# Preparing the walk over groups of 256 edges: one table of triples and 7 gathers for three tables and 21, links turned on TensorE, stores by single transfers

## The reference, cut to what matters

```python
edge_index = jnp.stack([src, dst])          # 200000 edges, dst sorted
alpha = leaky_relu(a_s[src] + a_d[dst], 0.2)
amax = segment_max(alpha, dst)              # softmax over the edges of one dst
e = exp(alpha - amax[dst]); z = segment_sum(e, dst)
out = segment_sum(xh[src] * (e / (z[dst] + 1e-16)), dst) + bias
```

## Time and profile before

| | |
|---|---|
| median of 3 runs | 7640.53 us |
| lowest and highest of them | 7630.43 and 7646.57 us |
| profiled execution, its own time | 7630.02 us |
| its span, first to last instruction | 7628.1 us |
| POOL, DVE, PE busy | 68%, 66%, 72% |

### The profile page before, as it was taken

How to read it: one execution, slowest core, us unless ns; L and a number is a source line. 1 busy time by engine, 2 the same in 40 slices (tenths; PEclk the granted TensorE clock), 3 DMA queues, 4 the chain that set the end, 5 groups by cost and what they waited for, 6 DMA issues and landing times. The chain is left out here.

```text
span 7628.1 us, 113689 instructions
## 1 busy us (share of the span) xinstructions
PE 5472.0 (72%) x23859; PEld 3659.4 (48%) x23860; DVE 5062.0 (66%) x13667; ACT 2560.3 (34%) x7905; POOL 5154.9 (68%) x5441
## 2 busy tenths in 40 slices
PE   3577777777666577777777776578888877774399
PEld 1254544544444355555544444355555544443398
DVE  4466666666667577777766667567777776668643
ACT  1322222222222333334332222344444432222466
POOL 1577777777774677777777773677777777772444
PEclk6777777777778777777777677677778777776599
DMA  4555555545453444444444444444444444444444
GB/s 117 160 145 141 145 144 142 145 136 140 139 139 101 121 120 121 123 123 122 123 116 112 112 111 117 125 124 126 129 127 128 129 120 112 112 111 128 150 70 64
DMA packets 547396, 947.74 MB, mean 124 GB/s; under 512 B 127840, under 2 KB 380808, under 8 KB 546759
## 3 DMA queue, kind: packets, MB, share of 16 engines
q0 software_dynamic: 260256, 691.84, 34.5%
q1 hardware_dynamic: 283255, 247.26, 10.9%
q10 hardware_dynamic: 3296, 2.36, 0.1%
HBM read 794.88 MB, written 149.50 MB: 124 GB/s over the span
## 5 line engine op out<-in xcount | busy, mean ns | idle before, releaser
L1213 POOL DMA_INDIRECT edges_G<-rows,edges_index x4980 | 4720.9, 948 | 1660.0 <-issue 1485.0
L1425 PE MATMUL edges_ps_o<-edges_G,edges_OH 128*128 128x264 f32 x9960 | 3542.1, 505 | 1233.2 <-DVE acc L1684 1230.3
L1425 PEld LDWEIGHTS edges_ps_o<-edges_G,edges_OH 128*128 128x128 f32 x9960 | 2300.0, 248 | 2009.3 <-DVE acc L1684 1394.9
L1263 ACT ACTIVATE edges_OHT<-edges_ps_far 128x512 bf16<-128x512 f32 x1245 | 741.0, 595 | 2305.0 <-PE edges_ps_far L1385 2304.9
L1666 DVE TENSOR_TENSOR edges_G<-edges_G,edges_ps_c 128x1024 f32<-128x1024 f32 x1245 | 1503.0, 1207 | 0.0
L1684 DVE TENSOR_TENSOR acc<-acc,edges_ps_o 128x264 f32 x2490 | 1059.8, 426 | 296.7 <-DVE acc L1684 161.6
L1565 DVE TENSOR_TENSOR edges_tu<-edges_ad,edges_G 128x80 f32<-128x80 f32 x249 | 75.0, 301 | 1252.5 <-DMA edges_G<-rows,edges_index 1252.5
L1658 DVE TENSOR_TENSOR edges_OH<-edges_ps_c,relT 128x512 f32<-128x512 f32 x1245 | 845.3, 679 | 0.6 <-ACT edges_ps_c L1240 0.5
L1385 PE MATMUL edges_ps_far<-edges_rels,pole_rows 5*128 5x512 bf16 x1245 | 608.4, 489 | 328.0 <-ACT edges_OHT L1263 285.3
L1385 PEld LDWEIGHTS edges_ps_far<-edges_rels,pole_rows 5*128 5x128 bf16 x1245 | 117.3, 94 | 959.4 <-issue 497.7
L1232 ACT ACTIVATE edges_node<-terms 128x12 bf16 x2490 | 476.2, 209 | 142.5 <-issue 88.4
(11 more groups left out here) (360 smaller groups left out, 6073.1 us busy)
## 6 DMA issues: line engine op xcount, KB each, us to landing
edges_G<-rows,edges_index POOLq DMA_INDIRECT x4980
xslot<-edges_blank SPq DMA_DIRECT2D x80, 650.0 KB
edges_masks<-lanes SPq DMA_DIRECT2D x249, 96.0 KB
rows<-node_ext SPq DMA_DIRECT2D x147, 130.0 KB, 2.3
experts_X<-xslot SPq DMA_DIRECT2D x105, 130.0 KB, 2.1
node_rows<-rows SPq DMA_DIRECT2D x98, 130.0 KB, 2.3
h<-node_Hn SPq DMA_DIRECT2D x98, 128.0 KB, 1.7
W<-in_L_ffn_W SPq DMA_DIRECT2D x16, 512.0 KB
```

The lines of the kernel that those rows point to most:

```text
L1213: g.indirect_dma_start(G[n][:, s, 0:RW], None, dr["rows"], bass.IndirectOffsetOnAxis(index[n][:, s:s + 1], 0)).then_inc(gathered[n], 16)
L1263: a.activation(OHT[:, 4 * k:4 * k + 4, :].rearrange("p s e -> p (s e)"), ps_far[:, :], ACT.Relu, bias=1.0, scale=-1.0).then_inc(oht_ready, 1)
L1425: mm = pe.matmul(ps_o[BANK_OF[g]][:, 0:GW], OH[:, 2 * g + j, :], G[n][:, 2 * g + j, :], start=(j == 0), stop=(j == 1))
```

## The change

The walk is rewritten in these points.

- `dstI` is loaded straight from the input `dst`, in three transfers, with no wait for a padded table.
- ACT's queue, which had nothing to do in this phase, builds one table `triples` of 783 rows, each 256 `dst`, 256 `dst` shifted by one and 256 `src` (3 KB a row), by ten transfers. POOL waits for them as well before it gathers, and issues 7 gathers of 3 KB a row into `Tg`.
- `ps_col` is no longer summed: DVE copies row 0 of `ps_row` out, and PE turns it by 7 matmuls of one column.
- DVE reads the gathered integers without the casts of both `dst` parts. The lanes' last flags (`edge_ends`) are turned on PE (4 transposes), so that `links` lies on 7 partitions with 256 numbers in a row.
- `cont`, `links`, `lanes` and `powers` are stored by one or two transfers each, `lanes` and `powers` on ACT's queue. `powers` lies in DRAM by group now, so that each edge window's `rels` load reads 30 pieces of 512 bytes in place of 3 of 5 KB.

```diff
+            sp.dma_start(dstI[:, 0:TC - 1, :], dst[0:full * GE].rearrange("(c p e) -> p c e", p=P, e=GE)).then_inc(dst_in, 16)
...
+            sp.dma_start(dr["cont"][1:1 + GC * GE].rearrange("(c p) -> c p", p=GE), links[:, 0, 1, :]).then_inc(cont_out, 16)
+            sp.wait_ge(cont_out, 32)
+            sp.dma_start(links[:, 1, 1, :], dr["cont"][0:GC * GE].rearrange("(c p) -> c p", p=GE)).then_inc(cont_in, 16)
             sp.wait_ge(links_ready, 2)
             for k in range(2):
-                for m in range(2):
-                    for c, n in chunks():
-                        sp.dma_start(by_lane(dr["links"][k, m, :], c, n), links[0:n, k, m, c, :]).then_inc(walk_out, 16)
+                sp.dma_start(dr["links"][k].rearrange("m (c p) -> c m p", p=GE), links[:, k, :, :]).then_inc(walk_out, 16)
...
+        @block.scalar
+        def _(a):
+            for m, (of, o) in enumerate(sources):
+                a.dma_start(triples[0:whole, m, :], of[o:o + whole * GE].rearrange("(t e) -> t e", e=GE)).then_inc(edges_in, 16)
...
+            a.wait_ge(lanes_ready, 3)
+            a.dma_start(dr["lanes"].rearrange("(c p j) x -> p c (j x)", p=P, j=2), lanes[:, :, :, :, :].rearrange("p c j m e -> p c (j m e)")
+                        ).then_inc(walk_out, 16)
...
+            g.wait_ge(edges_in, 16 * 10)
             g.wait_ge(index_ready, 1)
             for c in range(GC):
...
+                g.indirect_dma_start(Tg[:, c, :, :].rearrange("p a b -> p (a b)"), None, triples.rearrange("t a b -> t (a b)"),
+                                     bass.IndirectOffsetOnAxis(grpI[:, c:c + 1], 0)).then_inc(rows_in, 16)
...
+            for r in range(HALVES):
+                v.tensor_copy(row_grp[:, r * rowT:(r + 1) * rowT], ps_row[0:1, r, 0:rowT]).then_inc(row_ready, 1)
...
-            for m in range(GC):
-                for c in range(TC):
-                    mm = pe.matmul(ps_col[:, m:m + 1], passed[:, c, m * P:(m + 1) * P], ones[:, 0:1],
-                                   start=(c == 0), stop=(c == TC - 1))
             mm.then_inc(walked, 1)
+            pe.wait_ge(row_ready, 1 + HALVES)
+            for m in range(GC):
+                mm = pe.matmul(ps_col[:, m:m + 1], row_grp[:, m * P:(m + 1) * P], st["ident"][0:1, 0:1], start=True, stop=True)
+            mm.then_inc(row_turned, 1)
...
-                sp.dma_start(rels[r:r + 3, :], dr["powers"][:, bass.ds(w * WS * P, WS * P)]).then_inc(rels_in[w % 2], 16)
+                sp.dma_start(rels[r:r + 3, :].rearrange("k (v e) -> k v e", e=GE), dr["powers"][bass.ds(w * WG, WG), :, :].rearrange("v k e -> k v e")).then_inc(rels_in[w % 2], 16)
```

More of the change, by code:

```diff
@@ L127, in prepare_walk @@
     pad_rows = TG + 1
+    whole = E // GE
+    rest = E - whole * GE
+    assert 1 < rest < GE and whole + 1 == TG
     with Phase(nc, "walk") as ph:
-        pads = pad_rows * GE - E
-        cut = (E - 1) // 16 * 16
-        pad = ph.sb("pad", [1, 3, pads + 1], I32)
+        pad = ph.sb("pad", [1, 3, GE], I32)
         dstI = ph.sb("dstI", [P, TC, GE], I32)
@@ L195, in prepare_walk @@
         block = ph.block()
[L196 to L210, removed]
+        HALVES = 2
+        rowT = NG // HALVES
@@ L212, in _ @@
+        assert NG % HALVES == 0 and rowT <= 512
+        triples = dr["triples"]
+        sources = ((dst, 0), (dst, 1), (src, 0))
         @block.sync
         def _(sp):
[L214 to L224, removed]
@@ L234, in _ @@
+            sp.dma_start(dstI[whole - full:whole - full + 1, TC - 1, 0:rest], dst[whole * GE:E].rearrange("(a e) -> a e", a=1)
+                         ).then_inc(dst_in, 16)
             sp.wait_ge(pole_ready, 3)
@@ L248, in _ @@
[L248 to L255, removed]
@@ new lines, in _ @@
+            lane = lanes[:, :, :, :, :]
+            by_lane = nodes.rearrange("p c (j e) -> p c j e", j=2)
+            v.tensor_scalar(lane[:, :, :, 0, :], last[:, :, :].rearrange("p c (j e) -> p c j e", j=2), -BIG, None, ALU.mult
+                            ).then_inc(lanes_ready, 1)
+            for j in range(2):
+                for m, edge in ((1, 0), (2, P - 1)):
+                    v.tensor_tensor(lane[:, :, j, m, :], by_lane[:, :, j, :], by_lane[:, :, j, edge:edge + 1].broadcast_to([P, GC, P]),
+                                    ALU.is_equal).then_inc(same, 1)
@@ new lines, in _ @@
+            v.wait_ge(same, 4)
+            for m in (1, 2):
+                v.tensor_scalar(lane[:, :, :, m, :], lane[:, :, :, m, :], 1.0, BIG, ALU.subtract, ALU.mult).then_inc(lanes_ready, 1)
+            v.memset(before[:, :], -BIG).then_inc(cont_ready, 1)
+            v.wait_ge(lanes_ready, 3)
+            for m in range(2):
+                v.tensor_copy(edge_ends[:, m, :, :].rearrange("p j c -> p c j"), lane[:, :, :, m, P - 1]).then_inc(ends_ready, 1)
+            v.wait_ge(rows_ready, 3)
```

167 lines of the change are left out of this document (74 added, 93 removed).

## The result

| | before | after |
|---|---|---|
| median, lowest, highest of 6 runs | 7640.85, 7630.43, 7646.57 us | 7579.46, 7571.98, 7584.42 us |
| profiled execution: own time, span | 7630.02, 7628.1 us | 7579.77, 7578.0 us |
| next phase begins at | 125.45 us | 67.58 us |

The change takes 0.992 of the time before, 95% interval [0.991, 0.9929]. The forecast was 7579, the range 7565 to 7600.

The account below looks back on a forecast made before the run. POOL's gathers pace the edge phases, untouched by the change; the walk's 125 us, one chain, are all there is to win. Terms sum to -57.7 us, put on the mean 7636.9: 7579, range 7565 to 7600.

Parts of the forecast that it names:

- the load of `dstI`: Start of the walk: issued first, sharing engines evenly with the table copies, DVE begins at 9.3 for 16.08; -6.8 us.
- to the first gather: From DVE's first cast to POOL's first gather: pole rows moved, 49 column matmuls gone, copies and 7 matmuls added; -0.1 us.
- the table: ACT's copies of the triples land at 13 to 16 us, before gathers at 22.4; cost 0. Rival, late table: 7586, chance 0.08.
- the gathers: Walk, 7 gathers for 21 at POOL's 1.25 us each: 11.5 us for 28.8, -17.3. Rival, by bytes: 7596, chance 0.08.
- DVE on the rows: DVE's work after the gathers: two casts of 1.0 us go, small operations of 1.4 us come; net -0.6 us.
- the shifted links: DVE's idle wait for `cont` stored and loaded back: the lag of 4-byte pieces and the idle time go; -8.2 us.
- the end: From DVE's last copy to the next phase: stores land before DVE ends, 1.9 us remain of 26.6; -24.7 us.
- The upper bound: Load of `dstI`: DVE begins at 16.08, as now, if the load has to let all the table copies go first.
- 0.2 for two more hand-overs: Part of the stretch to the first gather: 0.2 us added for two more hand-overs.
- small stores stay slow: Rival: any small store to DRAM keeps the 9.4 us lag, DVE idles 4.4 us for the links; 7585, chance 0.22.
- 830 pieces against 8: Argument against slow small stores: `cont` went out in 830 4-byte pieces, now 7 rows of 512 bytes and one number.
- Later: Edge phases: `rels` loads of 30 pieces for 3 in each of 249 windows are hidden by a whole window; cost nothing.

Follow-up runs that it names:

- the later session: The change once more, unedited, beside the kernel before on the same chip: 7587.37 us, 0.9928 of 7643.65.
- 768 rows: The change with each large copy of the table cut into one of 768 rows and one of 13: 8951.07 us in one run, beside 9015.13 before.
- the kernel of 21 gathers: The change with three tables of 1 KB rows for one of triples, so 21 gathers: 7596.11 us, 0.9955 of 7630.11.
- 1792 pieces of 512 bytes: The change with ACT's shares, turns moved up, ACT doing all 42 copies, `powers` stored in three parts, a memset after POOL's table wait: 8949.19 us, 0.9928 of 9015.13.
- the old layout: The change with `powers` stored as before by three transfers, and three `rels` pieces a window: 7587.46 us, 0.9924.

## Why the prediction was right, step by step

The profiled executions of before and after, each stretch by its two ends:

| step | forecast | measured |
|---|---|---|
| the load of `dstI` (16.08 to 6.77) | -6.8 | -9.3 |
| to the first gather (13.22 to 14.19) | -0.1 | +1.0 |
| the table | 0 | 0 |
| the gathers (28.78 to 12.76) | -17.3 | -16.0 |
| DVE on the rows (23.35 to 23.39) | -0.6 | 0.0 |
| the shifted links (8.23 of idle time) | -8.2 | -8.2 |
| the 42 copies (9.19 to 9.37, with the last add) | 0 | +0.2 |
| the end (26.6 to 1.10) | -24.7 | -25.5 |
| sum | -57.7 | -57.9 |

The total is right to 0.2 us in the walk, and each of the large terms comes from the mechanism that was forecast, but the total flatters the sum: three terms were off by 1 to 2.5 us, and cancel. That the median is met to 0.5 us is luck. The medians lie 61.4 us apart, the profiled spans 50.1 and the two medians of the later session 56.3, and the change's own runs spread over 12 and 22 us.

**The load of `dstI`.** Taken in the middle of its bounds, by an even split with the copies, at 9.3; it was 6.77, near the lower bound of 6.3. "If the engines split their time evenly" did not hold, since the copies kept to 11 of the 16 engines (by their 0.69 of the rate of 768 rows). With 768 rows the cast came at 8.20, so up to 1.4 of the 2.5 us are that. The other 1.1 were there with 16 engines too, and what they come from isn't shown. The upper bound was a real one: with long packets in the copies it was 12.69.

**To the first gather.** The seven turns were priced at 1.33 from the upper row and took 1.72. "0.2 for two more hand-overs" was the step that failed: POOL's first gather now waits for the table and the index both, and that alone cost 0.6.

**The table.** It had landed by 16.07, the upper edge of the 13 to 16, 4.9 us before it was needed. The windows show copies that keep to 0.69 of what they reach with 768 rows (265 and 386 GB/s). The rule of the Trainium skill that the prediction weighed, 11 engines for 781 rows, is borne out by that, and the table came a microsecond ahead of the estimate by it. That it still landed near the sum's own 13 to 16 is two errors that cancel: 11 engines carried the copies where 16 were counted, and a piece took some 46 ns of an engine where 57 were (an estimate from the windows: 265 GB/s at a share of 0.75, and 386 at 1.09, give the same). As the prediction says, it left the sum alone; that it would help the load was not seen.

**The gathers.** POOL's pace was right (1.25 from the third gather on, 24.18 to 29.21), and so was the remark that the bytes lie close. They lay closer to binding than the 11.5 us had it. The windows of the changed kernel late in the gathers:

```profile
26.00:28.00 2.00, 0.00 (x0) 0.00 (x0) 0.00 (x0) 0.00 (x0) 1.39 (x3) 0.50 0.81 261
...
30.00:32.00 2.00, 0.00 (x0) 0.00 (x0) 0.00 (x0) 0.00 (x0) 0.16 (x1) 0.50 0.91 320
```

The share climbs to 0.91 and stays there when POOL has issued its last (29.21 and 0.95), and with rows of 1 KB (the kernel of 21 gathers) the tail is 3.1 us: the 1.1 us by which it grew (4.5 for 3.42) are bytes. The first two gathers, 3.2 us from the first's start to the third's for 2.5, give the rest.

**DVE on the rows.** The new cast of `Sf` reads every third run of `Tg` and takes 2.01 us, where the cast of a whole tile takes 1.09. The prediction counted casts by number, not by the form of their source. That is 0.9 us; the operations that were added took some 1.0 us and not 1.4, which gives part of it back.

**The shifted links and the end.** Both lags went, as the landing of 512-byte rows took 1.3 us, and the rival "small stores stay slow" was wrong: its 2-byte store did not lag. But the argument against it, the count ("830 pieces against 8"), is only half of the reason. The lag does not shrink from 3320 pieces to 830, and 1792 pieces of 512 bytes did not have it, so the count alone does not explain it. The end took 1.1 and not 1.9 us: `powers` and `links` had landed, and the earlier trace rows was read at too late a row. The first instruction of the phase that begins there is not DVE's at 252.85 but this one:

```profile
252.42 0.55 ACT L1224 ACTIVATE edges_index<-srcT 128x20 int32<-128x20 f32 x4 [7.30 <-PEq L104]
```

So that boundary took 1.2 us (251.22 to 252.42), not 1.6, and the margin on top wasn't needed.

**Later.** Costed at nothing, and nothing in one more execution of each kernel and in the old layout speaks against that. "It waits for nothing but issue" says a little more than the earlier trace rows do: 1485.0 of 1660.0 us are issue. The other 175 are, by the waits of the whole trace, 143.9 us at the start of the three edge phases and 31.1 us of waits for TensorE of at most 0.3 us, and they are the same with the change (144.5 and 31.4).

## What to carry to other kernels

When a phase is one chain, write it as a row of timestamps (first cast, first gather, last gather landed, last copy, next phase): each part of an edit then has its own two ends, and errors that cancel in the total can be seen. Look at the stores last: 28 stores of 4-byte pieces and the lag behind them cost 26.6 us of 125, more than the gathers gave, and turning the data first, so that each row goes out whole, took that to 1.1. When one load is needed early beside a bulk copy, the copy's spread and packet size set the load's time (6.77, 8.20 or 12.69 us here), and the fastest copy was not the best one for the load.

## What the runs showed that was not expected

- Behind stores of 4-byte pieces SP waits 7.8 to 10.6 us after its last issue, whatever their number (7, 14, 28 transfers) and spread, and no packet is recorded for the last 4.7 to 8.6 us of it. Behind 1792 pieces of 512 bytes it is 1.2 to 1.7 us from the last packet to the next phase.
- An indirect DMA that waits for a DMA and for DVE begins 1.10 us after DVE's instruction, and 0.46 when the first wait was taken by a memset before it.
- A cast from a source in separated runs takes 2.01 us, from a whole one 1.09.
- A copy of 781 rows keeps to 0.69 of the bandwidth of one of 768, and the load on another queue beside it is through 1.2 to 1.5 us earlier.
- One session's kernel before ran at 7630 us, another's on the same chip at 9015, and one on another chip at 9069, with the walk unchanged; the gathers' waits for loads and TensorE were longer. The runs do not say why.
